# A two-block graph attention kernel: the last two chunks' share of conv2's scores made apart from the features

## The chip, the cores and the metric

One core of one Trainium2 chip. The metric is the device time of one execution in microseconds (us). The kernel before has a median of 359.05 us over three runs (358.48, 359.05, 359.10); smaller is better.

## The reference, cut to what matters

256 nodes with 768 features, 4096 edges and a self loop for each node. Block 0 is two attention convolutions, conv1 with 8 heads of 768 channels and conv2 with one head; a layer norm and block 1 (two more convolutions with residual products) follow.

```python
def gat_conv(x, src, dst, W, a_src, a_dst, b, heads, out_ch):
    h = (x @ W).reshape(n, heads, out_ch)
    alpha_src = jnp.einsum('nhc,hc->nh', h, a_src)
    alpha_dst = jnp.einsum('nhc,hc->nh', h, a_dst)
    e = leaky_relu(alpha_src[src] + alpha_dst[dst], 0.2)
    p = jnp.exp(e - segment_max(e, dst)[dst])
    alpha = p / segment_sum(p, dst)[dst]
    return segment_sum(h[src] * alpha[:, :, None], dst).reshape(n, heads * out_ch) + b
# block 0
h = elu(gat_conv(x, src, dst, W1, a_src1, a_dst1, b1, 8, 768))
out = gat_conv(h, src, dst, W2, a_src2, a_dst2, b2, 1, 768)
x = layernorm(x + out)
```

W1 is 768 x 6144 and W2 is 6144 x 768, in float32. The scores alpha_src and alpha_dst of conv2 are dot products of each row of h @ W2 with a vector of 768; such a dot product can also be taken as h times (W2 times the vector), for all rows of W2 or for some of them.

## The kernel before, in words

**Number format.** Every large product takes three passes over operands split in a high part (rounded to fp32r) and a low part (what is left): high x high, high x low, low x high. ScalarE makes the high part by a copy and a following engine subtracts it from the source for the low part.

**Weights.** SyncE loads pairs of 128-row chunks of 768 columns into the three groups of `raw` (`load_phase`, L540; its issue L538). ScalarE splits a chunk into `ring_hi` (`split_hi`, L349, issued at L357), GpSimd makes `ring_lo` (`split_lo`, L367, issued at L370). A group is loaded again once GpSimd is done with its second chunk. A phase is six chunks: phase 2h-1 holds head h's part of W1 (phase 0 head 0's), phase 2h head h-1's part of W2, and phase 15, the last of block 0, head 7's part of W2. `split_hi` waits for a free ring slot, `chunk_used` counting the chunks that TensorE is done with.

**A head.** For head h TensorE projects x on six chunks (`project_chunk`, L1026), VectorE takes the two score dots from PSUM (L1515), TensorE broadcasts the source scores (`scores`, L1049), ScalarE and VectorE make the softmax, TensorE transposes the weights (L1075) and aggregates transposed features (`aggregate_T`, L1091, issued at L1096). `elu` (ScalarE L787, VectorE L1646) turns that in three parts of two chunks into zT: ScalarE relu (L794) and exp (L800), VectorE L1657, ScalarE `zT_hi` (L808), VectorE `zT_lo` (L1666). TensorE adds zT times the part of W2 into three PSUM banks that hold conv2's projected features of all heads so far (`accumulate`, L1039). The first projected chunk of head h+1 writes PSUM's third bank only after part 0 of head h's elu is out of it (`bank2_wait` in `project_chunk`, on `z_lo_done`). Heads 2 to 7 are loops or copies of a loop; heads 0 and 1 and ScalarE's head 7 are written out.

**The accumulator banks.** Tile 0 (nodes 0 to 127) has its columns 0:512 in the first bank and 512:768 in the second, tile 1 its columns 0:256 in the second and 256:768 in the third. In `product` (L999) a tile is two pieces, so a chunk costs six matmuls per tile: three of 512 columns and three of 256.

**The end of block 0.** After head 7's aggregation TensorE adds phase 15's six chunks to tile 0, then the 512-column pieces of tile 1, then its 256-column pieces (`last_accumulate`, L1241 to L1265). Behind each of these VectorE takes the dots (L1515, L1764). Then come `scores` (L1060), twelve matmuls of zeros (`keep_warm`, L1024, called at L1271), the leaky relu (ScalarE L764, VectorE L1571), the mask and row maximum (L1581), the exponential (ScalarE L773), its product with the edge counts (L1594), the transposed weights (`weights_tiles`, L1087; split by ScalarE L785 and VectorE L1643), and `aggregate` (L1118, issued at L1130), tile by tile and in each tile first the 512 columns, then the 256. Its results are scaled and summed on VectorE (`y_piece`, L1795), centred (ScalarE L907, VectorE L1805), transposed on TensorE (L1282), split (ScalarE L913, VectorE `x1_lo` L1788), and block 1's first products begin (`wide_product`, L1298). ScalarE converts features with `projected_tile_hi` (L738), VectorE with `conv2_lo` (L1750). Block 1's weights go through the same ring in 40 chunks of a written plan (`chunks_hi` L379, `split_lo1` L386).

**Rows for later.** Seven vectors of block 1 are loaded over all partitions behind the edge counting (L574, L576, semaphore `rows_loaded`); one of them is split into `bias_rows` by ScalarE (L883) and VectorE (L1756) after head 7. Both inputs of L1756 lie in SBUF. Most other VectorE instructions with two tensors read at least one from PSUM.

## Time and profile before

| what | value |
|---|---|
| median of three runs | 359.05 us |
| the profiled execution, its own time | 358.43 us |
| its span in the trace | 356.6 us |
| TensorE busy | 347.9 us (98%) |
| GpSimd busy | 242.4 us (68%) |
| ScalarE busy | 218.5 us (61%) |
| VectorE busy | 213.4 us (60%) |
| conv2's last products, first to last | 242.56 to 255.56 us |
| conv2's aggregation begins | 260.70 us |

The span is what the trace covers; the execution's own time is 1.83 us longer. TensorE's records are matmuls in a pipeline, so the start of one to the start of the next is its price and its listed duration is longer than that. Matmuls on zeros count as busy. In a timeline a line gives start, duration, engine and the line of the kernel; the bracket is the idle time before it and what ended it.

### The profile page before, as it was taken

To read this page: it belongs to the slowest core of one execution; us is meant where nothing else is said; L and a number is where in the kernel's file an instruction comes from. 1 tells how busy PE (TensorE), PEld (TensorE's weight loads), DVE (VectorE), ACT (ScalarE), POOL (GpSimd) and SP (SyncE) were. 2 spreads that over 40 slices of the span, in tenths; PEclk is the share of its full clock that TensorE was granted. 3 is DMA by queue.
4 is the path that set the end of the run, shared out by engine and by line. 5 is a ranking of instruction groups with operands and counts; after the bars stand their busy time and mean duration, and the time that the engine had idled before them with its cause. 6 is when DMAs were issued, how large, how long until landed. Compare 5 with 4: busy or idle time off the path is not lost.

```text
span 356.6 us, 6079 instructions
## 1 busy us (share of the span) xinstructions
PE 347.9 (98%) x2058; PEld 298.9 (84%) x2060; DVE 213.4 (60%) x545; ACT 218.5 (61%) x376; POOL 242.4 (68%) x163
## 2 busy tenths in 40 slices
PE   7999999999999999999999999999999999999994
PEld 4888889889888988988898898898667888788883
DVE  4999883263546418244552732636687897944776
ACT  5987697547737754864674575476376866255601
POOL 2379769657693884968569396674257898687911
PEclk9999999999999999999999999999999999999999
DMA  7987969576656556656574754757072656246002
GB/s 235 312 299 225 391 214 257 179 240 144 227 150 203 176 155 205 170 176 183 170 217 143 224 170 141 246 159 237 11 218 94 217 179 198 99 135 221 0 2 88
DMA packets 24544, 65.15 MB, mean 183 GB/s; under 512 B 1952, under 2 KB 3024, under 8 KB 24528
## 3 DMA queue, kind: packets, MB, share of 16 engines
q1 hardware_dynamic: 20864, 55.02, 47.0%
q10 hardware_dynamic: 3664, 9.92, 10.8%
q8 instruction: 9, 0.15, 0.2%
q14 instruction: 7, 0.06, 0.0%
HBM read 64.15 MB, written 0.79 MB: 182 GB/s over the span
## 4 chain that ended last, share of the span: by engine, by line
PE 92%; DVE 4%; ACT 1%; DMA 1%; issue 1%; DVEq 0%; SPq 0%
PE ps L1008 64%; PE ps L1298 10%; PE ps L1096 9%; PE ps L1130 2%; PE ps L1362 2%; PE ps L1075 1%; DMA x_sb<-in_x 1%; PE ps L1060 1%; PE ps L1192 1%; DVE stats L1744 1%; DVE ps L1964 1%; DVE z L1971 1%; PE ps L1157 0%; PE ps L1383 0%; PE ps L1310 0%
## 5 line engine op out<-in xcount | busy, mean ns | idle before, releaser
L370 POOL TENSOR_TENSOR ring_lo<-raw,ring_hi 128x768 fp32r<-128x768 f32 x92 | 167.0, 1849 | 70.9 <-ACT ring_hi L357 70.8
L357 ACT ACTIVATE ring_hi<-raw 128x768 fp32r<-128x768 f32 x96 | 77.3, 839 | 35.7 <-PE ps L1008 28.8
L386 POOL TENSOR_TENSOR ring_lo<-raw,ring_hi 128x512 fp32r<-128x512 f32 (+1 forms) x40 | 59.5, 1517 | 20.3 <-ACT ring_hi L379 20.2
L1008 PE MATMUL ps<-ring_hi,zT_hi 128*128 128x256 f32 (+1 forms) x256 | 69.3, 345 | 0.4 <-ACT zT_hi L808 0.4
L1008 PE MATMUL ps<-ring_lo,zT_hi 128*128 128x256 f32 (+1 forms) x256 | 67.1, 337 | 0.0
L1008 PE MATMUL ps<-ring_hi,zT_lo 128*128 128x256 f32 (+1 forms) x256 | 66.8, 338 | 0.0
L1515 DVE CUSTOM_DVE_ANT_0 e<-ps,att 128x768 f32<-128x768 f32 x38 | 34.3, 953 | 47.6 <-PE ps L1008 47.6
L1008 PE MATMUL ps<-ring_hi,xT_hi 128*128 128x512 f32 x192 | 51.2, 343 | 0.3 <-ACT xT_hi L702 0.3
L1008 PE MATMUL ps<-ring_lo,xT_hi 128*128 128x512 f32 x192 | 50.0, 336 | 0.0
L1008 PE MATMUL ps<-ring_hi,xT_lo 128*128 128x512 f32 x192 | 49.8, 337 | 0.0
L1008 PEld LDWEIGHTS ps<-ring_lo,zT_hi 128*128 128x128 f32 x256 | 43.0, 188 | 5.6
L1008 PEld LDWEIGHTS ps<-ring_hi,zT_lo 128*128 128x128 f32 x256 | 43.0, 188 | 5.5
L1008 PEld LDWEIGHTS ps<-ring_hi,zT_hi 128*128 128x128 f32 x256 | 42.0, 189 | 6.4 <-ACT zT_hi L808 1.0
L379 ACT ACTIVATE ring_hi<-raw 128x512 fp32r<-128x512 f32 (+1 forms) x40 | 26.5, 712 | 17.0 <-PE ps L1008 10.0
L1657 DVE SCALAR_TENSOR_TENSOR ps<-ps,b_plus,z 128x256 f32<-128x256 f32 x48 | 21.2, 487 | 25.9 <-ACT z L800 25.8
L1008 PEld LDWEIGHTS ps<-ring_hi,xT_hi 128*128 128x128 f32 x192 | 32.3, 188 | 5.0 <-ACT xT_hi L702 0.7
L1008 PEld LDWEIGHTS ps<-ring_lo,xT_hi 128*128 128x128 f32 x192 | 32.7, 188 | 4.2
L1008 PEld LDWEIGHTS ps<-ring_hi,xT_lo 128*128 128x128 f32 x192 | 32.6, 188 | 4.1
L1096 PE MATMUL ps<-pT_hi,h_hi 128*128 128x256 f32 x96 | 26.0, 282 | 0.0
L1096 PE MATMUL ps<-pT_hi,h_lo 128*128 128x256 f32 x96 | 26.0, 282 | 0.0
L1666 DVE SCALAR_TENSOR_TENSOR zT_lo<-ps,zT_hi 128x512 fp32r<-128x512 f32 x24 | 16.6, 691 | 15.3 <-ACT zT_hi L808 15.3
L794 ACT ACTIVATE z<-ps,b_minus 128x256 f32<-128x256 f32 x48 | 20.1, 471 | 6.2 <-PE ps L1096 6.2
(172 smaller groups left out, 545.4 us busy)
## 6 DMA issues: line engine op xcount, KB each, us to landing
raw<-in_L_gnn_W SPq DMA_DIRECT2D x54, 768.0 KB, 4.5
raw<-in_L_gnn_Wr SPq DMA_DIRECT2D x8, 768.0 KB, 4.3
att<-in_L_gnn_a_src ACTq DMA_DIRECT2D x10, 384.0 KB, 4.0
att<-in_L_gnn_a_dst ACTq DMA_DIRECT2D x10, 384.0 KB, 5.2
raw<-in_L_gnn_W SPq DMA_DIRECT2D x4, 384.0 KB, 5.0
x_sb<-in_x SPq DMA_DIRECT2D x3, 256.0 KB, 4.8
...
```

The lines of the kernel that those rows point to most:

```text
L357: eng.activation(slot_hi(c), raw_chunk(c), ACT.Copy).then_inc(hi_done, 1)
L370: eng.tensor_tensor(slot_lo(c), raw_chunk(c), slot_hi(c).bitcast(F32), ALU.subtract)\
L379: eng.activation(ring_hi[:, q["ring_at"]:q["ring_at"] + w], raw[:, q["raw_group"], q["raw_at"]:q["raw_at"] + w], ACT.Copy)\
L386: eng.tensor_tensor(ring_lo[:, q["ring_at"]:q["ring_at"] + w], raw[:, q["raw_group"], q["raw_at"]:q["raw_at"] + w], ring_hi[:, q["ring_at" ...
L794: act.activation(z[:, t * N:(t + 1) * N], ps[:, at:at + N], ACT.Relu, bias=b1_minus[:, bass.ds(KD * h + t, 1)], scale=-1.0).then_inc(elu_r ...
L1008: last = pe.matmul(ps[:, at + to:at + to + hi - lo], a, b[:, lo:hi], start=start and n == 0 and to != D, stop=stop and n == PASSES - 1, sk ...
L1096: return pe.matmul(ps[:, at:at + N], feat(features, 0, j)[:, ch:ch + P], weights_part[:, 0, j, :], start=first, stop=final, skip_group_che ...
L1130: return pe.matmul(ps[:, nat_at[i] + lo:nat_at[i] + hi], weights_part[:, 0, j, i * P:(i + 1) * P], feat(features, a, j)[:, lo:hi], start=f ...
L1298: last = pe.matmul(ps[:, to:to + HW], a, b, start=k == 0 and n == 0, stop=k == KD - 1 and n == PASSES - 1, skip_group_check=True)
L1515: dve.tensor_tensor_reduce(junk[:, at:at + w], of[:, (k - first_head(a)) * w:(k - first_head(a) + 1) * w], att[:, half_at * row + k * w:ha ...
L1657: dve.scalar_tensor_tensor(ps[:, at:at + N], ps[:, at:at + N], b1_plus[:, bass.ds(KD * h + t, 1)], z[:, t * N:(t + 1) * N], ALU.add, ALU.m ...
L1666: dve.scalar_tensor_tensor(zT_lo[:, 2 * q:2 * q + 2, :].rearrange("p k n -> p (k n)"), ps[:, at:at + 2 * N], -1.0, hi.bitcast(F32), ALU.ad ...
```

## The change

Chunks 4 and 5 of phase 15 get a second way into the scores. GpSimd multiplies these two raw chunks with the two attention vectors spread over the partitions (`weigh_rows`, four instructions of 128 x 768), ScalarE sums their rows (`row_sum`, four), and the four columns are split and multiplied with zT (`late_rows`), turned into columns (`late_columns`) and added to the dots that VectorE takes from the accumulator after chunks 0 to 3 (`ends`). TensorE then adds chunks 4 and 5 bank by bank around the broadcast of the scores. The twelve matmuls of zeros go. conv2's aggregation is ordered by feature tile instead of by column piece. The attention vectors are loaded a second time, early, by SyncE. The split of `bias_rows` moves from behind head 7 to head 1.

The diff, without declarations, with the leading eight spaces and some plain lines left out:

```diff
+att2 = hs[:, 0:2 * D]
+ZV_AT, ZV_COLS_AT = 0, N
+LATE = (KD - 2, KD - 1)
...
+def weighted_row(m):
+    at = 2 * N + (m % 2) * D
+    return am[:].rearrange("p a b c -> p (a b c)")[:, at:at + D]
...
+def src_col(a, k, j):
+    if isinstance(a, int) and a == A_CONV2 and j == 0:
+        return ends[:, 0:1]
+    return a_s[:, pair(a, k, j)]
+def dst_col(a, k, i):
+    if isinstance(a, int) and a == A_CONV2 and i == 0:
+        return ends[:, 1:2]
+    return a_d[:, pair(a, k, i)]
...
+    sp.wait_ge(unpacked, 2)
+    for n, v in enumerate((b0_as2, b0_ad2)):
+        sp.dma_start(att2[:, n * D:(n + 1) * D], v[0:1, :].partition_broadcast(P)).then_inc(att2_loaded, 16)
     with sp.Fori(2, H0) as h:
         load_phase(2 * h - 1, w1_of(h))
         load_phase(2 * h, w2_of(h - 1))
...
-    with pool.Fori(1, H0) as h:
+    with pool.Fori(1, H0 - 1) as h:
         head(h)
+    def weigh_rows(c):
+        for half_at in range(2):
+            m = 2 * LATE.index(c) + half_at
+            if m >= 2:
+                pool.wait_ge(attw_done, m - 1)
+            pool.tensor_tensor(weighted_row(m), raw_chunk(c), att2[:, half_at * D:(half_at + 1) * D], ALU.mult)\
+                .then_inc(weighted_done, 1)
+    phase_lo(PHASES - 2)
+    pool.wait_ge(raw_full[LATE[0] // 2], 16 * PHASES)
+    pool.wait_ge(att2_loaded, 32)
+    weigh_rows(LATE[0])
+    for c in range(LATE[0]):
+        split_lo(pool, PHASES - 1, c)
+    weigh_rows(LATE[1])
+    for c in LATE:
+        split_lo(pool, PHASES - 1, c)
...
+        if last:
+            after_exps(h, between=lambda: (row_sum(0), row_sum(1)))
+            elu(h, between=lambda: row_sum(2))
+            row_sum(3)
+        else:
+            after_exps(h)
+            elu(h)
+    def row_sum(m):
+        act.wait_ge(weighted_done, m + 1)
+        act.activation(weighted_row(m), weighted_row(m), ACT.Copy, scale=SLOPE - 1.0 if m % 2 else 1.0,
+                       accum_out=attw[:, m:m + 1]).then_inc(attw_done, 1)
+    def after_exps(h, between=None):
         for c in range(4):
             split_hi(act, 2 * h + 1, c)
         weights_hi(h)
+        if between is not None:
+            between()
         for c in (4, 5):
             split_hi(act, 2 * h + 1, c)
...
     att_for(2)
+    act.wait_ge(rows_loaded, 16 * 7)
+    for half_at in range(2):
+        act.activation(bias_rows[half_at], rows_hc[0:BIAS_ROWS, 3, half_at * HW:(half_at + 1) * HW], ACT.Copy)\
+           .then_inc(bias_row_hi, 1)
     elu(1)
     with act.Fori(2, H0 - 1) as h:
         head(h)
     head(H0 - 1, last=True)
-    act.wait_ge(rows_loaded, 16 * 7)
-    for half_at in range(2):
-        act.activation(bias_rows[half_at], rows_hc[0:BIAS_ROWS, 3, half_at * HW:(half_at + 1) * HW], ACT.Copy)\
-           .then_inc(bias_row_hi, 1)
+    act.wait_ge(attw_done, 4)
+    act.activation(attw_hi[:, :], attw[:, :], ACT.Copy).then_inc(attw_hi_done, 1)
     act.wait_ge(xb_done, NT)
     act.dma_start(rows_d[:, 3, :], b1_br2.partition_broadcast(P)).then_inc(rows_loaded, 16)
...
-    act.wait_ge(a_dst_done, before(A_CONV2) + 1)
-    projected_tile_hi(A_CONV2, 0)
+    act.wait_ge(zv_rows_ps, 1)
+    act.activation(zv_rows[:, :], ps[0:2, ZV_AT:ZV_AT + N], ACT.Copy).then_inc(zv_rows_done, 1)
     chunks_hi(0, 2)
     leaks(A_CONV2)
+    chunks_hi(2, 3)
+    exps(A_CONV2, (0, 1))
+    act.wait_ge(tile0_done, 1)
+    projected_tile_hi(A_CONV2, 0)
+    weights_tiles_hi(A_CONV2)
+    act.wait_ge(chunk_used, CH * PHASES)
+    act.wait_ge(h_lo0_done, before(A_CONV2) + 1)
     projected_tile_hi(A_CONV2, 1)
-    exps(A_CONV2, (0, 1))
-    chunks_hi(2, 3)
     load_att(A_GAT1A, b1_as1.rearrange("h c -> (h c)"), b1_ad1.rearrange("h c -> (h c)"), HC)
-    weights_tiles_hi(A_CONV2)
...
     pe.wait_ge(z_lo_done, 3 * (H0 - 1) + 1)
     for c in (0, 1):
         last_accumulate(c, 0, passes=LAST_ONE)
-    for q in (1, 2):
-        pe.wait_ge(z_hi_done, 3 * (H0 - 1) + q + 1)
-        for c in (2 * q, 2 * q + 1):
-            chunk(PHASES - 1, c)
-            last_accumulate(c, 0, passes=FIRST_TWO)
-        pe.wait_ge(z_lo_done, 3 * (H0 - 1) + q + 1)
-        for c in (2 * q, 2 * q + 1):
-            last = last_accumulate(c, 0, passes=LAST_ONE)
+    pe.wait_ge(z_hi_done, 3 * (H0 - 1) + 2)
+    for c in (2, 3):
+        chunk(PHASES - 1, c)
+        last_accumulate(c, 0, passes=FIRST_TWO)
+    pe.wait_ge(z_lo_done, 3 * (H0 - 1) + 2)
+    for c in (2, 3):
+        last = last_accumulate(c, 0, passes=LAST_ONE)
+    last.then_inc(early_bank_done, 1)
+    for c in range(LATE[0]):
+        last = last_accumulate(c, 1, piece=0)
+    last.then_inc(early_bank_done, 1)
+    def late_rows():
+        pe.wait_ge(z_lo_done, 3 * H0)
+        pe.wait_ge(attw_lo_done, 1)
+        for c in LATE:
+            at = 2 * LATE.index(c)
+            for n, (a, b) in enumerate(three(attw_hi[:, at:at + 2], attw_lo[:, at:at + 2],
+                                             zT_hi[:, c, :], zT_lo[:, c, :])):
+                last = pe.matmul(ps[0:2, ZV_AT:ZV_AT + N], a, b, start=c == LATE[0] and n == 0,
+                                 stop=c == LATE[1] and n == PASSES - 1)
+        last.then_inc(zv_rows_ps, 1)
+    def late_columns():
+        pe.wait_ge(zv_rows_done, 1)
+        for i in range(NT):
+            at = ZV_COLS_AT + 2 * i
+            last = pe.transpose(ps[:, at:at + 2], zv_rows[:, i * P:(i + 1) * P], ident[0:2, 0:2])
+        last.then_inc(zv_ps, 1)
+    for c in range(LATE[0]):
+        if c == 2:
+            late_rows()
+        if c == 3:
+            late_columns()
+        last_accumulate(c, 1, piece=1).then_inc(chunk_used, 1)
+    pe.wait_ge(partial_done, 2)
+    for c in LATE:
+        chunk(PHASES - 1, c)
+        if c == LATE[1]:
+            last_accumulate(c, 0, piece=0, passes=(0,))
+            scores(A_CONV2)
+            last_accumulate(c, 0, piece=0, passes=(1, 2))
+        else:
+            last_accumulate(c, 0, piece=0)
+    pe.wait_ge(partial_done, 4)
+    pe.wait_ge(a_dst_done, before(A_CONV2) + 1)
+    for c in LATE:
+        last_accumulate(c, 0, piece=1)
+        last = last_accumulate(c, 1, piece=0)
     last.then_inc(tile0_done, 1)
-    for c in range(CH):
-        last = last_accumulate(c, 1, piece=1)
-    last.then_inc(wide_piece_done, 1)
-    pe.wait_ge(h_lo0_done, before(A_CONV2) + 1)
-    for c in range(CH):
-        last_accumulate(c, 1, piece=0).then_inc(chunk_used, 1)
-    pe.wait_ge(z_lo_done, 3 * H0)
-    idle = PROJ + BANK
-    scores(A_CONV2)
-    keep_warm(12, idle)
+    pe.wait_ge(a_dst_done, before(A_CONV2) + 2)
+    for c in LATE:
+        last_accumulate(c, 1, piece=1).then_inc(chunk_used, 1)
+    def aggregate_conv2():
+        def part(i, j, weights_part, features, first, final):
+            done = None
+            for lo, hi in NAT_PIECES:
+                done = pe.matmul(ps[:, NAT_AT[i] + lo:NAT_AT[i] + hi], weights_part[:, 0, j, i * P:(i + 1) * P],
+                                 feat(features, A_CONV2, j)[:, lo:hi], start=first, stop=final)
+                if final:
+                    done.then_inc(conv2_done, 1)
+        for i in range(NT):
+            pe.wait_ge(wt_hi_done, i + 1)
+            pe.wait_ge(h_hi_done, before(A_CONV2) + 1)
+            if i == 1:
+                pe.wait_ge(h_lo0_done, before(A_CONV2) + NT)
+            part(i, 0, pT_hi, h_hi, True, False)
+            pe.wait_ge(h_lo0_done, before(A_CONV2) + 1)
+            part(i, 0, pT_hi, h_lo, False, False)
+            pe.wait_ge(wt_lo_done, i + 1)
+            part(i, 0, pT_lo, h_hi, False, False)
+            pe.wait_ge(h_hi_done, before(A_CONV2) + NT)
+            part(i, 1, pT_hi, h_hi, False, False)
+            part(i, 1, pT_lo, h_hi, False, False)
+            pe.wait_ge(h_lo0_done, before(A_CONV2) + NT)
+            part(i, 1, pT_hi, h_lo, False, True)
     weights_tiles(A_CONV2)
-    aggregate(A_CONV2)
+    aggregate_conv2()
...
     weights_lo(1)
+    dve.wait_ge(bias_row_hi, 2)
+    for half_at in range(2):
+        row = bias_rows[half_at][32:33, :]
+        dve.tensor_tensor(row, rows_hc[32:33, 3, half_at * HW:(half_at + 1) * HW], row.bitcast(F32),
+                           ALU.subtract).then_inc(bias_row_done, 1)
     elu(1)
     with dve.Fori(2, H0) as h:
...
+    conv2_sum_done = (a_src_done, a_dst_done)
+    def piece_dots(i, cols, initial, to, done):
+        of = source_at(A_CONV2, i)[:, cols]
+        for half_at in range(2):
             junk = (e1, e2)[half_at][:].rearrange("p a b c -> p (a b c)")
-            to = partial[:, half_at:half_at + 1] if initial is None else t[:, 1:2]
-            dve.tensor_tensor_reduce(junk[:, D + cols.start:D + cols.stop], of,
+            dve.tensor_tensor_reduce(junk[:, i * D + cols.start:i * D + cols.stop], of,
                                      att[:, half_at * D + cols.start:half_at * D + cols.stop],
                                      SLOPE - 1.0 if half_at else 1.0,
                                      0.0 if initial is None else initial[:, half_at:half_at + 1],
-                                     ALU.mult, ALU.add, to).then_inc(done[half_at], 1)
-    tile_dots(A_CONV2, 0)
-    conv2_lo(0)
-    dve.wait_ge(wide_piece_done, 1)
-    piece_dots(slice(N, D), None, (partial_done, partial_done))
-    projected(A_CONV2, 1)
+                                     ALU.mult, ALU.add, to[half_at]).then_inc(done[half_at], 1)
+    dve.wait_ge(att_loaded, 32 * (A_CONV2 + 1))
+    dve.wait_ge(early_bank_done, 1)
+    piece_dots(0, slice(0, BANK), None, [partial[:, n:n + 1] for n in (4, 5)], (partial_done, partial_done))
+    dve.wait_ge(attw_hi_done, 1)
+    dve.tensor_tensor(attw_lo[:, :], attw[:, :], attw_hi[:, :].bitcast(F32), ALU.subtract).then_inc(attw_lo_done, 1)
+    dve.wait_ge(early_bank_done, 2)
     dve.wait_ge(partial_done, 2)
-    piece_dots(slice(0, N), partial, (a_src_done, a_dst_done))
+    piece_dots(0, slice(BANK, D), partial[:, 4:6], [partial[:, n:n + 1] for n in (0, 1)], conv2_sum_done)
+    piece_dots(1, slice(0, N), None, [partial[:, n:n + 1] for n in (2, 3)], (partial_done, partial_done))
+    dve.wait_ge(a_src_done, before(A_CONV2) + 1)
+    dve.wait_ge(a_dst_done, before(A_CONV2) + 1)
+    dve.wait_ge(partial_done, 4)
+    dve.wait_ge(zv_ps, 1)
+    dve.tensor_tensor(ends[:, :], ps[:, ZV_COLS_AT:ZV_COLS_AT + 4], partial[:, 0:4], ALU.add).then_inc(zv_added, 1)
+    dve.wait_ge(zv_added, 1)
+    dve.wait_ge(chunk_used, CH * (PHASES - 1) + LATE[0])
+    piece_dots(1, slice(N, D), ends[:, 2:4], [t[:, 1:2] for t in (a_s, a_d)], conv2_sum_done)
     masked_scores(A_CONV2)
     weigh(A_CONV2, 0)
     weigh(A_CONV2, 1)
-    conv2_lo(1)
+    conv2_lo(0)
     weights_tiles_lo(A_CONV2)
     inverse_sums(A_CONV2)
+    conv2_lo(1)
```

## Rows read from the trace of the kernel before

**Rows 1.** Chain of waits, end of block 0: start us, us, what

```profile
242.56 13.01 PE ps L1008 x72
...
256.23 0.42 PE ps L1060 x2
...
259.70 0.45 PE ps L1087 x2
...
260.70 4.43 PE ps L1130 x24
```

**Rows 2.** Table of windows: busy us of each engine, clock, DMA share, GB/s

```profile
255.56:260.70 5.14, 3.76 (x17) 1.77 (x19) 3.92 (x15) 3.44 (x8) 2.04 (x3) 1.00 0.10 37
```

**Rows 3.** Timeline of TensorE, conv2's last products

```profile
249.10 0.39 PE L1008 MATMUL ps<-ring_hi,zT_hi 128*128 128x512 f32 x1
...
253.21 0.32 PE L1008 MATMUL ps<-ring_hi,zT_hi 128*128 128x256 f32 x1
```

**Rows 4.** Timeline of ScalarE, head 7 up to its elu

```profile
232.92 3.05 ACT L357 ACTIVATE ring_hi<-raw 128x768 fp32r<-128x768 f32 x4 [0.50 <-issue]
...
236.35 0.83 ACT L357 ACTIVATE ring_hi<-raw 128x768 fp32r<-128x768 f32 x1
...
239.33 0.84 ACT L794 ACTIVATE z<-ps,b_minus 128x256 f32<-128x256 f32 x2 [0.58 <-PE ps L1096]
```

**Rows 5.** Timeline of GpSimd, phase 15

```profile
233.84 10.88 POOL L370 TENSOR_TENSOR ring_lo<-raw,ring_hi 128x768 fp32r<-128x768 f32 x6 [5.48 <-ACT ring_hi L357]
```

**Rows 6.** Tile raw, 225 to 245 us: SyncE's issues, time to landing

```profile
L538 SPq DMA_DIRECT2D raw<-in_L_gnn_W x2: 368/373/378, 224.8 to 228.4; - x2
...
DMA to landing us min/median/max: 4.2/4.4/4.6
```

**Rows 7.** Timeline of VectorE, end of block 0

```profile
253.41 0.69 DVE L1764 CUSTOM_DVE_ANT_0 e<-ps,att 128x512 f32<-128x512 f32 x1 [0.32 <-PE ps L1008]
...
259.95 0.95 DVE L1750 TENSOR_TENSOR h_lo<-ps,h_hi 128x768 fp32r<-128x768 f32 x1
...
264.46 0.76 DVE L1795 SCALAR_TENSOR_TENSOR ps<-ps,rz,x_sb 128x512 f32<-128x512 f32 x1
...
266.41 1.01 DVE L1788 TENSOR_TENSOR xT_lo<-ps,xT_hi 128x512 fp32r<-128x512 f32 x2
```

**Rows 8.** Timeline of ScalarE, conv2's features and weights

```profile
257.40 0.81 ACT L738 ACTIVATE h_hi<-ps 128x768 fp32r<-128x768 f32 x1
...
260.17 0.77 ACT L785 ACTIVATE pT_hi<-ps 128x256 fp32r<-128x256 f32 x2
```

**Rows 9.** Timeline of ScalarE: head 1 up to its elu; later the bias rows

```profile
50.31 3.04 ACT L357 ACTIVATE ring_hi<-raw 128x768 fp32r<-128x768 f32 x4
...
56.54 0.89 ACTq L685 DMA_DIRECT2D att<-in_L_gnn_a_dst  x1
57.59 0.84 ACT L794 ACTIVATE z<-ps,b_minus 128x256 f32<-128x256 f32 x2 [0.22 <-PE ps L1096]
...
246.76 0.62 ACT L883 ACTIVATE zT_hi<-rows_hc 33x512 fp32r<-33x512 f32 x1
```

**Rows 10.** Timeline of VectorE, part 0 of head 1's zT_lo

```profile
60.68 0.69 DVE L1666 SCALAR_TENSOR_TENSOR zT_lo<-ps,zT_hi 128x512 fp32r<-128x512 f32 x1 [0.67 <-ACT zT_hi L808]
```

**Rows 11.** Timeline of TensorE: head 1's aggregation, head 2 in the third bank

```profile
55.97 0.28 PE L1096 MATMUL ps<-pT_hi,h_hi 128*128 128x256 f32 x1
...
61.67 0.39 PE L1008 MATMUL ps<-ring_hi,xT_hi 128*128 128x512 f32 x1
```

**Rows 12.** DMA issues from 35 to 40 us (KB each, us to landing)

```profile
raw<-in_L_gnn_W SPq DMA_DIRECT2D x1, 768.0 KB, 11.3
```

**Rows 13.** Table of windows, 40 to 42 us (columns as in rows 2)

```profile
40.00:42.00 2.00, 2.00 (x17) 1.90 (x17) 1.88 (x5) 1.74 (x5) 1.92 (x2) 1.00 1.02 411
```

**Rows 14.** Timeline of VectorE, the bias rows behind head 7

```profile
247.93 0.68 DVE L1756 TENSOR_TENSOR zT_hi<-rows_hc,zT_hi 1x512 fp32r<-1x512 f32 x1 [0.34 <-ACT zT_lo L883]
```

**Rows 15.** Timeline of GpSimd, head 1

```profile
47.48 14.63 POOL L370 TENSOR_TENSOR ring_lo<-raw,ring_hi 128x768 fp32r<-128x768 f32 x8 [5.56 <-ACT ring_hi L357]
```

51 lines of the change are left out of this document (22 added, 29 removed).

## The prediction

> **What bounds the kernel now.** I read the page first: TensorE is busy 98% of the span, so only two kinds of time can be won, TensorE's gaps and work that TensorE does for nothing. The chain of waits shows where it is not TensorE that counts [rows 1]: conv2's last products run 13.0 us without a break, then between the last of them (255.56) and the aggregation (260.70) the chain goes through VectorE's last dots, the broadcast of the scores, the softmax and the transposes. The table of windows for that stretch [rows 2] says that TensorE was busy 3.76 of 5.14 us, but the work that counts there is six transposes, 0.42 + 0.45 us [rows 1]; the rest of the busy time is zeros. So about 4.3 us are open, and the most that a better order can give is that.
>
> **What the change puts in the gap.** The prices of TensorE's instructions are distances of starts [rows 3]: from 249.10 to 253.21 there are 18 matmuls of 512 columns, 0.228 us each, and 18 matmuls of 256 columns follow up to the end of the products at 255.56, at most 0.13 us each; without the longer end of the last one it is 0.122. The dots need chunks 0 to 3 only. What is left behind the third bank's chunk 3 is chunks 4 and 5: 12 x 0.228 + 12 x 0.122 = 4.2 us. That is the cover; I follow each step to see whether it holds. All times are on the clock of the profiled execution.
>
> *The start.* ScalarE gets two row sums between the weights of head 7 and its splits of chunks 4 and 5. Splits follow one another every (3.05 - 0.83) / 3 = 0.74 us and the next one began at 236.35; relu began at 239.33 [rows 4]. Two row sums and two splits take 4 x 0.74 = 2.96 us and end at 239.31, just in time. What a row sum's accumulator costs is on no row; VectorE's read of its own is listed with 0.08 to 0.14 us, so I take 0.12 each, between 0 and 0.3: elu and with it the first product come 0.25 us late.
>
> *GpSimd.* It was idle for 5.48 us before phase 15 [rows 5]. The third group was issued at 228.4 and takes 4.3 us to land [rows 6], so the first two multiplications can start at 232.75. I price a multiplication like a split of the same shape, 10.88 / 6 = 1.81 us: both are done at 236.4, splits 0 to 3 at 243.7, the other two multiplications at 247.3, splits 4 and 5 at 249.1 and 251.0. TensorE wants chunk 3 at 242.8 + 12 x 0.175 = 244.9 (0.175 is the mean of the two prices, as a chunk has both pieces) and chunks 4 and 5 at 252.5 and 253.2, so nothing waits, with one microsecond to spare. The last row sum is then ready at about 248.3 and its split at 249.4; `late_rows` is reached at 242.8 + 24 x 0.175 + 12 x 0.122 + 6 x 0.228 = 249.8. This is the tightest point (margin 0.4).
>
> *Scores.* `late_rows` adds 6 x 0.122 = 0.7 us and `late_columns` two transposes of two columns, at 0.1 to 0.2 us each, plus a wait of some 0.15 for ScalarE's copy. The third bank's chunk 3 ends at 252.7. The dot of 512 columns takes 0.69 us [rows 7]; TensorE does four matmuls meanwhile and waits 0.1 us. The scores are broadcast at 253.6 and not 256.23, so weights come at 259.70 - 2.6 = 257.1. TensorE's products end at 242.8 + 12.84 (the 13.01 less the 0.17 by which a last end lies behind the next start) + 0.7 for the rows + 0.3 for the columns + 0.3 of waits + 0.44 for the broadcast = 257.4. The softmax is hidden, and the transposes begin at 257.4 instead of 259.70: 2.3 us gained here.
>
> *The aggregation.* Here part of it is given back. Before, one copy and one low part of the features lay before the gap and the rest in it. Now all are behind the products: ScalarE copies a tile in 0.81 us and splits two weight tiles in 0.77 [rows 8], VectorE needs 0.95 per low part [rows 7], and the second copy waits for the first low part. From the transposes: weights split 258.3, low part of tile 0 258.7, copy of tile 1 259.6, low part of tile 1 260.6. The passes of tile 0 hang on these and end at about 261.1; tile 1 follows with six passes of 0.35 us and ends at 263.2 against 265.1 [rows 1]. Also, both column pieces of a tile now end together, so VectorE begins tile 1's sum only 0.35 + 0.15 us earlier than the last product's end: at about 263.2 where it was 264.46 [rows 7]. The end of `x1_lo` is what block 1's first products wait for, and it moves as this does. If the copies of this chain follow closer than I think the gain is 1.6 us, if looser 0.9. I take 1.3 us. Behind it the chain is nearly all TensorE (92% of the whole chain), so the 1.3 us reach the end. The zeros cost nothing and their removal gives nothing by itself: they ended before the transposes.
>
> **The bias rows.** ScalarE's two copies (0.62 each, overlapping by 0.1 as the splits do) and VectorE's two subtractions move before head 1's elu. Behind head 7 they were hidden. In head 1 ScalarE's last issue of a DMA ended at 57.43 and relu began at 57.59 [rows 9], so relu moves to 57.45 + 2 x 0.52 = 58.5, 0.9 us later. The exponential and VectorE's two steps are a chain behind it. Part 0 of `zT_lo` ended at 61.37 [rows 10], and TensorE's first matmul on the third bank, which needs it, began at 61.67 [rows 11]: 0.30 us of slack, of which 0.05 to 0.15 is the semaphore's. TensorE stalls 0.65 us there (between 0.5 and 0.9), and as it works without gaps until head 7 nothing gives that back.
>
> **The second load of the attention vectors.** Two more transfers of 384 KB stand on SyncE's queue ahead of phase 3's first group, which landed 11.3 us after its issue because the queue was full [rows 12]; at 411 GB/s [rows 13] 0.79 MB are 1.9 us more. Group 0 then lands at 38.5 + 11.3 + 1.9 = 51.7; group 1, which follows it in the full queue, some 1.8 us later at 53.5. ScalarE's four splits began at 50.31 and ended at 53.35 [rows 9]; they now end at 55.1, the copy of the weights at 55.6. TensorE began the aggregation that wants it at 55.97 [rows 11]. I cost that at nothing, with 0.3 us left; at 1 us more delay it is 0.7. The wait for `unpacked` costs nothing, it is over before SyncE gets there. Declarations and GpSimd's unrolled head cost nothing that TensorE waits for.
>
> **Sum.** 358.43 - 1.3 + 0.65 = 357.8 on the profiled execution. That run was 0.62 us under the median, so on the median 358.4. A measurement tells 0.2% (0.72 us) from no change: the forecast is at the upper edge of what cannot be told. The range of this case alone is 357.8 to 359.1.
>
> **Rivals.**
> *1. VectorE and GpSimd get in each other's way (slower).* The moved subtractions read two tensors from SBUF. Behind head 7 they took 0.68 us with GpSimd idle [rows 14]; in head 1 GpSimd works from 47.48 without a break for 14.6 us on operations of 1.83 us that read SBUF too [rows 15]. No row has such a VectorE instruction beside a running GpSimd one. If each has to wait for one to end, the pair is late by 1 to 3.5 us, all of it ahead of head 1's elu; `attw_lo`, which also reads two tensors from SBUF while GpSimd splits chunk 4, can be late by up to 1.8 us with `late_rows` behind it, beyond the margin of 0.4. Stall in head 1: 1.3 to 3 us instead of 0.65, plus 0 to 1.4 in conv2. Taking 2.3 and 0.6: 359.05 - 1.3 + 2.3 + 0.6, about 360.6; it decides from 0.65 us of extra wait on. Its range is 359.3 to 361.5. For it: the type of operand; against it: no row shows one being held up. The Trainium skill (SBUF — State Buffer, section "SBUF: two separate sides") says just this: a VectorE instruction with two SBUF inputs and a GpSimd instruction that reads SBUF share a port pair as an exclusive lock, and whoever comes second is blocked for a whole instruction. The traces here neither confirm nor deny it. Chance 0.30.
> *2. The front costs nothing (faster).* ScalarE may reach the bias rows early or the chain behind relu be shorter than listed. Then the 1.3 us stand alone, up to 1.6: 357.75. The timeline is against it. Chance 0.17.
> *3. The gain fails in conv2.* The accumulator reads, the last row sum or the tile-wise chain of copies cost more: the scores come later than the products end, or tile 0's passes are late. With 1 us of the 1.3 lost: 359.4. Chance 0.13.
> The forecast keeps 0.40.
>
> **Numbers.** Of the forecast's 0.40 some 0.16 is faster by over 0.2%, 0.24 within. Rival 2 is faster; rival 1 gives 0.25 slower and 0.05 within; rival 3 0.09 within and 0.04 slower. Rounded: faster 0.34, within 0.37, slower 0.29. The range runs from rival 2 with its larger gain, 357.2, to the middle of rival 1, 360.6.
>
> **What would show it.** In the profile after: the scores' broadcast at about 253.6 + 0.65; transposes with no idle time before them; gaps of 0.1 to 0.5 us inside tile 0's aggregation; relu of head 1 near 58.5 and TensorE's stall on the third bank of 0.5 to 0.9 us (rival 2: none; rival 1: over 1.3, with VectorE's L1756 starting or lasting past its 0.68). I am wrong if `late_rows` waits for `attw_lo`, if head 1's aggregation starts late, or if block 1's first product comes less than 0.3 us or more than 2 us earlier relative to head 7's aggregation.

## The result: slower by 1.3%, and the profile after

The changed kernel takes 363.24 us (median of four runs, 362.24 to 365.08) where the kernel before, on the same chip, takes 359.03: a ratio of 1.0130 with a 95% interval of 1.0113 to 1.0147. The forecast was 358.4 with a range up to 360.6, so both the size and the direction were wrong. The profiled execution took 365.08 us with a span of 363.4. It is the longest of the four, 6.65 us over the profiled one of before, and the sums below are made on it.

| what | before | after |
|---|---|---|
| profiled execution, own time / span | 358.43 / 356.6 us | 365.08 / 363.4 us |
| mean granted TensorE clock of that execution | 1.000 | 0.988 |
| head 1's aggregation begins | 55.97 | 56.78 |
| first matmul on the third bank behind it | 61.67 | 65.94 |
| head 2's aggregation begins | 86.16 | 93.10 |
| conv2's last products begin | 242.56 | 249.58 |
| block 1's first product | 266.26 | 272.70 |

From head 1's aggregation on, the differences of the two columns are +0.81, +4.27, +6.94, +7.02 and +6.44. All of the loss is there when head 2's aggregation begins, at a quarter of the span; the end of block 0, which the change is about, gives 0.58 us back. The view to read first is therefore the list of TensorE's waits (kernel after; total us, times, longest):

```profile
PE ps L1083 <- DVE zT_lo L1794: 3.2, 1, 3.2
...
PE ps L1337 <- DVE attw_lo L1903: 0.8, 1, 0.8
PE ps L1171 <- ACT pT_hi L835: 0.6, 1, 0.6
```

The first is the third bank's matmul of head 2 waiting for head 1's elu, the second `late_rows` waiting for the low part of the four columns, the third head 1's aggregation waiting for its weights. The timeline of the kernel after in head 1 (start us, us) shows where the first comes from; it answers to [rows 9 to 11, 15]:

```profile
53.56 11.71 POOL L393 TENSOR_TENSOR ring_lo<-raw,ring_hi 128x768 fp32r<-128x768 f32 x6 [2.40 <-ACT ring_hi L380]
...
52.64 1.58 ACT L380 ACTIVATE ring_hi<-raw 128x768 fp32r<-128x768 f32 x2 [2.22 <-DMA raw<-in_L_gnn_W]
54.57 1.58 ACT L380 ACTIVATE ring_hi<-raw 128x768 fp32r<-128x768 f32 x2 [0.35 <-DMA raw<-in_L_gnn_W]
...
58.22 0.61 ACT L947 ACTIVATE zT_hi<-rows_hc 33x512 fp32r<-33x512 f32 x1
...
59.26 0.81 ACT L850 ACTIVATE z<-ps,b_minus 128x256 f32<-128x256 f32 x2
...
64.57 0.60 ACT L864 ACTIVATE zT_hi<-ps 128x512 fp32r<-128x512 f32 x1 [3.11 <-DVE ps L1785]
...
59.38 1.99 DVE L1855 TENSOR_TENSOR zT_hi<-rows_hc,zT_hi 1x512 fp32r<-1x512 f32 x1 [2.02 <-ACT zT_lo L947]
61.30 2.32 DVE L1855 TENSOR_TENSOR zT_lo<-rows_hc,zT_lo 1x512 fp32r<-1x512 f32 x1
63.65 0.89 DVE L1785 SCALAR_TENSOR_TENSOR ps<-ps,b_plus,z 128x256 f32<-128x256 f32 x2
65.19 0.69 DVE L1794 SCALAR_TENSOR_TENSOR zT_lo<-ps,zT_hi 128x512 fp32r<-128x512 f32 x1 [0.66 <-ACT zT_hi L864]
...
65.94 0.79 PE L1083 MATMUL ps<-ring_hi,xT_hi 128*128 128x512 f32 x1 [3.23 <-DVE zT_lo L1794]
```

The two subtractions of the bias rows, one partition by 512, take 1.99 and 2.32 us; behind head 7 the first took 0.68 [rows 14]. GpSimd is at work beside them without a break (53.56 to 65.27). Read one by one, its splits show who waits for whom: the first subtraction ends at 61.37, 0.55 us after the split that ran when it began (60.82), the second at 63.62, 0.55 us after the next one (63.07). And the two splits that start meanwhile last 2.28 and 2.24 us where the others of this stretch last 1.83 to 1.86. elu's first step on VectorE stands behind them, and TensorE behind elu. The steps of elu themselves keep their price (0.69 for L1794, as in [rows 10]), and they run beside the same GpSimd instructions.

What follows the wait is in the table of windows of the kernel after (us of the stretch, busy of PE, PEld, DVE, ACT, POOL, granted clock, DMA share, GB/s):

```profile
62.00:64.00 2.00, 0.71 (x6) 0.46 (x4) 1.97 (x2) 0.00 (x0) 2.00 (x2) 1.00 0.94 343
64.00:66.00 2.00, 0.06 (x1) 0.06 (x1) 1.34 (x4) 1.43 (x4) 1.28 (x1) 0.69 0.84 341
66.00:68.00 2.00, 2.00 (x5) 1.61 (x6) 1.34 (x4) 1.52 (x4) 0.00 (x0) 0.50 0.68 207
68.00:70.00 2.00, 2.00 (x9) 1.71 (x8) 1.34 (x4) 1.14 (x2) 0.00 (x0) 0.50 0.54 215
70.00:72.00 2.00, 2.00 (x9) 1.69 (x8) 0.18 (x1) 0.72 (x2) 1.73 (x1) 0.60 0.04 15
72.00:74.00 2.00, 2.00 (x13) 1.78 (x12) 0.00 (x0) 0.62 (x2) 1.71 (x2) 1.00 0.00 0
...
64.77:71.59 6.82, 5.65 (x16) 4.75 (x17) 3.66 (x7) 4.21 (x9) 1.83 (x2) 0.50 0.50 182
```

TensorE stood idle for 3.2 us, and when it begins again the granted clock is 0.50, the lower of its two levels (1.2 GHz). The last line is that whole stretch, 6.8 us, of which TensorE works 5.65. Busy reads 2.00 in the windows of 2 us all the same: only the count of matmuls (5 and 9 in place of 13) tells. From the third bank's first matmul to head 2's aggregation it takes 27.16 us and took 24.49: 2.7 us that no wait lists, and near half of the 5.65.

At the end of block 0 (timeline of the kernel after, answering to [rows 1, 7, 8]):

```profile
243.98 0.19 ACT L890 ACTIVATION_READ_ACCUMULATOR am<-am 128x1 f32 x1
...
254.00 3.64 POOL L393 TENSOR_TENSOR ring_lo<-raw,ring_hi 128x768 fp32r<-128x768 f32 x2
...
255.75 1.91 DVE L1903 TENSOR_TENSOR attw_lo<-attw,attw_hi 128x4 fp32r<-128x4 f32 x1
...
257.81 0.28 PE L1337 MATMUL ps<-zT_hi,attw_hi 128*2 128x256 f32 x1 [0.84 <-DVE attw_lo L1903]
...
261.42 0.32 PE L1135 MATMUL ps<-ident,ends 128*128 128x128 f32 x1
...
264.98 0.76 PE L1162 MATMUL ps<-ident,e 128*128 128x128 f32 x4
265.83 0.62 PE L1379 MATMUL ps<-h_hi,pT_hi 128*128 128x512 f32 x2
266.55 0.62 PE L1379 MATMUL ps<-h_lo,pT_hi 128*128 128x512 f32 x2
```

A subtraction of four columns lasts 1.91 us. Behind it everything goes as meant: the scores are broadcast (261.42) while products still run, there is no idle time before the transposes (264.98), the aggregation follows right behind them, and from the first of the last products to block 1's first product 23.12 us in place of 23.70, the wait of 0.84 included.

Theory 1 after this reading: a VectorE instruction with both inputs in SBUF is held up while GpSimd works. That makes the stall of 3.2 us and the 0.84 us before `late_rows`, and the idle TensorE loses its clock on top. The rivals: the loss comes from the second load's delay or from ScalarE's copies; it is the size of the instruction and not its operands that costs; and, for the clock, that it costs nothing of its own. Each expectation below stands as it was written before its run.

### The profile page after: what moved, and what is told of

It is laid out like the page before. It is cut to its first block, busy times and chain, and to the rows that moved or that the text cites. A ratio compares the mean times of both kernels' runs of the same rounds, so it can differ in the third digit from the quotient of the medians.

```text
span 363.4 us, 6088 instructions
## 1 busy us (share of the span) xinstructions
PE 351.2 (97%) x2056; PEld 300.5 (83%) x2056; DVE 218.6 (60%) x551; ACT 222.2 (61%) x386; POOL 250.6 (69%) x167
## 2 busy tenths in 40 slices
DMA packets 24833, 65.94 MB, mean 181 GB/s; under 512 B 1985, under 2 KB 3057, under 8 KB 24817
## 4 chain that ended last, share of the span: by engine, by line
PE 74%; DVE 8%; ACT 6%; issue 4%; POOL 4%; DMA 3%; ACTq 0%; DVEq 0%; SPq 0%; POOLq 0%
PE ps L1083 51%; PE ps L1426 9%; PE ps L1171 6%; POOL ring_lo L393 3%; ACT ring_hi L380 2%; PE ps L1490 2%; DMA raw<-in_L_gnn_W 1%; PE ps L1150 1%; DMA x_sb<-in_x 1%; PE ps L1135 1%; ACT h_hi L794 1%; DVE e L1643 1%; DVE stats L1877 1%; PE ps L1379 1%; DVE zT_lo L1855 1%
## 5 line engine op out<-in xcount | busy, mean ns | idle before, releaser
L1083 PE MATMUL ps<-ring_hi,zT_lo 128*128 128x512 f32 (+1 forms) x256 | 67.3, 338 | 0.0
L1643 DVE CUSTOM_DVE_ANT_0 e<-ps,att 128x768 f32<-128x768 f32 x36 | 32.4, 953 | 49.7 <-PE ps L1083 49.7
L1083 PE MATMUL ps<-ring_hi,xT_hi 128*128 128x512 f32 x192 | 52.4, 349 | 3.2 <-DVE zT_lo L1794 3.2
L1083 PE MATMUL ps<-ring_lo,xT_hi 128*128 128x512 f32 x192 | 50.9, 341 | 0.0
L1083 PE MATMUL ps<-ring_hi,xT_lo 128*128 128x512 f32 x192 | 50.7, 342 | 0.0
L1083 PEld LDWEIGHTS ps<-ring_hi,xT_hi 128*128 128x128 f32 x192 | 33.2, 193 | 8.6 <-DVE zT_lo L1794 3.4
L1794 DVE SCALAR_TENSOR_TENSOR zT_lo<-ps,zT_hi 128x512 fp32r<-128x512 f32 x24 | 16.6, 692 | 15.3 <-ACT zT_hi L864 15.3
L864 ACT ACTIVATE zT_hi<-ps 128x512 fp32r<-128x512 f32 x24 | 14.4, 598 | 14.8 <-DVE ps L1785 14.7
```

What stands on the lines that cost most here:

```text
L864: act.activation(zT_hi[:, 2 * q:2 * q + 2, :].rearrange("p k n -> p (k n)"), ps[:, at:at + 2 * N], ACT.Copy, bias=-1.0).then_inc(z_hi_done, 1)
L1083: last = pe.matmul(ps[:, at + to:at + to + hi - lo], a, b[:, lo:hi], start=start and n == 0 and to != D, stop=stop and n == PASSES - 1, sk ...
L1643: dve.tensor_tensor_reduce(junk[:, at:at + w], of[:, (k - first_head(a)) * w:(k - first_head(a) + 1) * w], att[:, half_at * row + k * w:ha ...
L1794: dve.scalar_tensor_tensor(zT_lo[:, 2 * q:2 * q + 2, :].rearrange("p k n -> p (k n)"), ps[:, at:at + 2 * N], -1.0, hi.bitcast(F32), ALU.ad ...
```

## The experiments

All ratios are against the kernel before on the same chip, whose median was 358.64 us in the runs of the first four, 358.63 in those of the next four and 358.83 in those of the last three.

**1. Only the bias rows moved, on the kernel before.**

```diff
-    (behind head 7) act: 2 x activation(bias_rows ...);  dve: 2 x tensor_tensor(row, rows_hc, row, subtract)
+    (head 1, before elu(1)) the same four instructions
```

> The kernel before with one part of the change alone: the split of the bias rows moved to head 1. Theory 1 (a VectorE instruction that reads two tensors from SBUF is held up by each running GpSimd instruction): L1756's two instructions last about 2 us each instead of 0.68, TensorE stalls 2.5 to 3.5 us at head 2's first chunk, and where the granted clock falls after it another 1 to 3 us go; time 361.5 to 365. Theory 2 (only the copies' 1.04 us delay relu, the forecast's term): both instructions stay at 0.7 us, stall 0.65 us, time about 359.7.

Measured 363.92 us (363.78 to 364.74), ratio 1.0153 (1.0137 to 1.0169). The timeline of VectorE:

```profile
58.69 2.18 DVE L1727 TENSOR_TENSOR zT_hi<-rows_hc,zT_hi 1x512 fp32r<-1x512 f32 x1 [3.31 <-ACT zT_lo L878]
60.80 2.30 DVE L1727 TENSOR_TENSOR zT_lo<-rows_hc,zT_lo 1x512 fp32r<-1x512 f32 x1
```

This move alone makes 5.3 us, more than the whole loss of 4.2. TensorE's wait on the third bank is 3.6 us.

**2. Only the second load of the attention vectors, on the kernel before.**

```diff
+    sp.wait_ge(unpacked, 2)
+    for n, v in enumerate((b0_as2, b0_ad2)): sp.dma_start(att2[...], ...)
     with sp.Fori(2, H0) as h:
```

> The kernel before with the second load of the attention vectors alone, early in SyncE's order. Theory 1 (the transfers in front delay phase 3's first groups past the slack): ScalarE's copy of head 1's weights ends about 0.8 us later than TensorE wants it, aggregation of head 1 starts 0.5 to 0.9 us late, time 359.6 to 359.9. Theory 2 (the forecast: inside the slack): no idle time before head 1's aggregation, time 359.0 within 0.3.

Measured 358.79 us (358.39 to 359.72), ratio 1.0009 (1.0000 to 1.0019). Head 1's aggregation begins at 55.99, as before. In the profile head 2's begins 0.34 us later than before (86.50 against 86.16), the median is 0.15 us up: alone the load costs little.

**3. The change with its front put back.** The bias rows are copied behind head 7 and subtracted by GpSimd after its third chunk of block 1; the second load stands before phase 15.

```diff
-    (head 1) act: 2 copies of bias rows;  dve: 2 subtractions
+    (behind attw_hi) act: 2 copies
+    pool (between chunks of block 1): 2 x tensor_tensor(row, rows_hc, row, subtract)
-    sp: att2 load before Fori(2, H0)
+    sp: att2 load before load_phase(PHASES - 1, ...)
```

> The changed kernel with both costs at the front taken out: the bias rows are copied behind head 7 and subtracted by GpSimd after its third chunk of block 1, the second load of the attention vectors stands before phase 15. Theory 1 (the whole loss lies in head 1, conv2 itself gains 0.6 us and pays 0.8 us for attw_lo): time 358.2 to 358.7, faster than before by 0.4 to 0.8. Theory 2 (the change also loses elsewhere, in block 1 or in the clock): 359.5 or more.

Measured 358.49 us, but from 357.46 to 359.69 over twelve runs; ratio 0.9992 (0.9978 to 1.0006). That is the time that theory 1 named, and the loss is gone; but against the kernel before on the same chip it is 0.15 us and not told from no change. In its profile `attw_lo` fell on the seam between two splits of GpSimd, which worked from 247.70 to 251.36 without a break:

```profile
247.70 3.66 POOL L393 TENSOR_TENSOR ring_lo<-raw,ring_hi 128x768 fp32r<-128x768 f32 x2
...
249.46 0.16 DVE L1906 TENSOR_TENSOR attw_lo<-attw,attw_hi 128x4 fp32r<-128x4 f32 x1
```

0.16 us here and 1.91 in the kernel after, for the same instruction at the same distance (6.17 us) from the first of the last products. In both kernels it is listed 0.06 us before the second split (249.51 here, 255.81 there). So at such a seam the listed times do not tell which of the two gets in first, and 1.75 us hang on it. Whether this makes the spread of 2.2 us was not seen, as no longer execution was profiled.

**4. The same, and ScalarE makes `attw_lo`.** ScalarE computes scale times input plus a bias per partition, one column at a time.

```diff
-    dve.tensor_tensor(attw_lo, attw, attw_hi, ALU.subtract)
+    for m in range(4):
+        act.activation(attw_lo[:, m:m + 1], attw_hi[:, m:m + 1], ACT.Identity, bias=attw[:, m:m + 1], scale=-1.0)
```

> As c_front_back, and the low part of the four weight columns is made by ScalarE (identity of minus the high part plus the column as bias) so that VectorE has no instruction with two SBUF inputs there. Theory 1: attw_lo no longer holds up VectorE for 1.9 us, TensorE's wait of 0.8 us before late_rows goes, time 0.7 to 0.9 us under c_front_back (357.4 to 357.8). Theory 2 (late_rows would have waited for the last row sum anyway): less than 0.3 us under c_front_back.

Measured 357.55 us (357.44 to 357.72), ratio 0.9970 (0.9958 to 0.9981): faster than both kernels, 1.1 us under before, with a spread of 0.28 us over six runs. From the first of the last products (242.76) to block 1's first product (264.89) it takes 22.13 us, 1.57 less than before; the latter comes 1.37 earlier. In experiment 3's profile, where `attw_lo` took its 0.16 us, that stretch took 22.14 us too, so the 0.94 us between the two medians lie in executions that no profile shows. That `attw_lo` makes them is the likely reading and not a shown one. TensorE's waits of this kernel behind the start:

```profile
PE ps L1095 <- ACT zT_hi L872: 0.5, 1, 0.5
PE ps L1095 <- ACT xT_hi L766: 0.3, 1, 0.3
...
PE ps L1422 <- ACT x_sb L994: 0.2, 1, 0.2
```

**5. The instruction by itself.** The kernel before with small VectorE instructions on idle tiles: in head 1 twice while GpSimd works, and once near the end, where it is idle (eleven in all).

```diff
+    dve.tensor_tensor(hs[512 columns], counts, far, ALU.add)           # two inputs in SBUF (L1727)
+    dve.tensor_tensor(hs[4 columns], counts, far, ALU.add)             # the same, 4 columns (L1728)
+    dve.tensor_scalar(hs[512 columns], counts, 1.0, None, ALU.add)     # one input (L1729)
+    dve.tensor_tensor(hs[512 columns], ps, counts, ALU.add)            # one in PSUM, not near the end (L1731)
```

> The kernel before with twelve small VectorE instructions added that compute nothing the output needs: a 128x512 sum of two SBUF tensors, a 128x4 sum of two SBUF tensors, a 128x512 add of a constant to one SBUF tensor and a 128x512 sum of one PSUM and one SBUF tensor, twice in head 1 while GpSimd works without a break, and the first three once near the end while GpSimd is idle. The time is no question here, the durations are. Theory 1 (the operands decide): beside GpSimd the two sums of SBUF tensors last until the running GpSimd instruction ends, 0.2 to 1.9 us longer than alone, the 4 column one as long as the 512 column one; the sum with a PSUM tensor keeps 0.69 us. Theory 2 (size decides, or it is the single partition of L1756): the 4 column sum stays at 0.2 us and the 512 column one near 0.7 us.

The tile's instructions (least, median, greatest ns), then the timelines of VectorE and GpSimd in head 1:

```profile
L1727 DVE TENSOR_TENSOR hs<-counts,far x3: 686/1112/1595, 52.7 to 346.6; 128x512 f32<-128x512 f32 x3
L1728 DVE TENSOR_TENSOR hs<-counts,far x3: 157/1754/1799, 53.7 to 347.2; 128x4 f32<-128x4 f32 x3
L1729 DVE TENSOR_SCALAR hs<-counts x3: 411/414/422, 55.5 to 347.3; 128x512 f32<-128x512 f32 x3
L1731 DVE TENSOR_TENSOR hs<-ps,counts x2: 675/676/676, 55.8 to 60.0; 128x512 f32<-128x512 f32 x2
```

```profile
52.69 1.11 DVE L1727 TENSOR_TENSOR hs<-counts,far 128x512 f32<-128x512 f32 x1
53.73 1.80 DVE L1728 TENSOR_TENSOR hs<-counts,far 128x4 f32<-128x4 f32 x1
55.45 0.41 DVE L1729 TENSOR_SCALAR hs<-counts 128x512 f32<-128x512 f32 x1
55.78 0.68 DVE L1731 TENSOR_TENSOR hs<-ps,counts 128x512 f32<-128x512 f32 x1
...
47.64 15.91 POOL L371 TENSOR_TENSOR ring_lo<-raw,ring_hi 128x768 fp32r<-128x768 f32 x8 [6.07 <-ACT ring_hi L358]
```

The execution took 366.26 us with its additions, a number that stands for nothing else. Four columns take 0.16 us with GpSimd idle and 1.75 to 1.80 beside it. So neither size nor the single partition decides but the operands: the same kind of instruction with one input in PSUM takes 0.68 beside GpSimd. Each of the two held sums of four columns ends 0.02 us after the split that ran beside it (55.53 after 55.50, 59.77 after 59.75): it waits for that split's end. GpSimd pays too: its eight splits took 15.91 us, and [rows 15] has 14.63. The splits that start while a sum of 512 columns waits last 2.30 and 2.24 us in place of some 1.85.

The instruction with a single SBUF input took 0.41 throughout; but it stood right behind one that had just waited for GpSimd, so these rows don't exclude that it would wait elsewhere. It isn't free for GpSimd either: the splits that begin 0.02 us after it last 2.07 and 2.06 us and end 1.67 to 1.68 us after it ends, as the others end 1.66 to 1.70 after a two-input one. It seems to hold GpSimd up as these do; no run has it alone.

**6. Only ScalarE's two copies in head 1**, the subtractions left behind head 7.

```diff
+    (head 1, before elu(1)) act: 2 x activation(bias_rows ...)
```

> The kernel before with ScalarE's two copies of the bias rows alone moved to head 1; VectorE subtracts behind head 7 as before. This is the forecast's own term for head 1. Theory 1 (relu 0.9 us later against 0.3 us of slack): TensorE stalls 0.5 to 0.9 us at head 2's first chunk in the third bank, time 0.4 to 0.9 us over before. Theory 2 (the chain takes it up): no stall, time within 0.2 of before.

Measured 359.96 us (359.70 to 360.15), ratio 1.0035 (1.0022 to 1.0048). Timeline of TensorE:

```profile
62.85 0.50 PE L1008 MATMUL ps<-ring_hi,xT_hi 128*128 128x512 f32 x1 [0.46 <-DVE zT_lo L1666]
```

The stall is 0.46 us, near the 0.65 that the prediction gave to the move; the time rose by 1.3. In this profile head 1's aggregation already begins 0.55 us late (56.52), behind longer waits for `ring_lo` and x. From there to the third bank's first matmul it takes 6.33 us and took 5.70, which is 0.63 more, and to head 2's aggregation 0.80 more. So the copies' price is between 0.5 and 1.3 us and not settled closer. The subtractions take the rest of the 5.3, about 4.

**7. The kernel before without its twelve matmuls of zeros.**

```diff
     scores(A_CONV2)
-    keep_warm(12, idle)
```

> The kernel before without the twelve matmuls of zeros between the scores and the transposes. Theory 1 (idle time of about 4 us lets the granted clock fall to 1.2 GHz, as the 3.2 us stall in the changed kernel did): conv2's aggregation and block 1's first products run at the lower clock for some us, time 1.5 to 4 us over before. Theory 2 (the forecast: the zeros cost and bring nothing): granted clock 1.00 in that stretch, time within 0.2 of before.

Measured 360.95 us (360.23 to 361.69), ratio 1.0065 (1.0053 to 1.0077). TensorE's wait before the transposes, and the table of windows:

```profile
PE ps L1087 <- DVE e L1593: 3.1, 1, 3.1
...
258.00:260.00 2.00, 0.00 (x0) 0.00 (x0) 1.87 (x9) 1.48 (x4) 0.00 (x0) 1.00 0.00 0
260.00:262.00 2.00, 1.81 (x7) 1.29 (x8) 1.93 (x6) 1.93 (x5) 1.44 (x2) 0.83 0.75 240
262.00:264.00 2.00, 2.00 (x7) 1.61 (x7) 0.21 (x1) 0.80 (x2) 2.00 (x2) 0.50 1.05 298
264.00:266.00 2.00, 2.00 (x11) 1.78 (x10) 1.62 (x6) 0.24 (x1) 1.60 (x2) 0.82 0.95 347
```

The wait before the transposes grows to an idle time of 3.1 us and the clock is at half behind it, for 3.4 us (261.30 to 264.72). Work that computes nothing was worth 2.3 us there by the medians, and 1.6 in this profile, the shortest of the six. The change can drop it only because its order closes the gap.

**8. Kernel 4 with the aggregation by column piece**, as it was before.

```diff
-    aggregate_conv2()      # tile by tile; tile 0's passes wait for tile 0's operands alone
+    by_piece()             # waits for both feature tiles, then 512 columns, then 256
```

> d_no_shared_port with conv2's aggregation in the order of the kernel before (512 columns, then 256, in each tile) instead of by feature tile. Theory 1 (the order by feature tile uses the time until the second copy and its low part are there): the aggregation starts about 1 us later and ends 0.5 to 0.9 us later, time 0.3 to 0.9 us over d_no_shared_port. Theory 2 (both wait for the same last low part): time within 0.2 of d_no_shared_port.

Measured 358.50 us (357.69 to 359.82), ratio 0.9998 (0.9984 to 1.0013). Timeline of TensorE:

```profile
259.79 0.50 PE L1419 MATMUL ps<-h_hi,pT_hi 128*128 128x512 f32 x1 [1.72 <-ACT h_hi L802]
```

From the first of the last products (242.90) to block 1's first product (265.40) it takes 22.50 us, only 0.4 more than kernel 4's 22.13, yet the median is 0.95 us up: of the twelve runs those of 357.7 to 358.0 us have a mean clock of 0.997 to 0.999, those of 359.0 to 359.8 one of 0.992 to 0.994. The profile is one of the short ones, so that the clock falls behind the idle time of 1.7 us is an inference from the means. If it holds, the order by tile is worth having for the idle time that it takes away, more than for its own 0.4.

**9, 10. Zeros in the stall of experiment 1, and its control.** Head 2 of TensorE is written out, so that zeros can stand there alone.

```diff
+    for _ in range(14):     # only in the first of the two, just ahead of the third bank's first matmul
+        pe.matmul(ps[:, PROJ:PROJ + BANK], zeros[:, 0:P], zeros[:, :], start=False, stop=False)
```

> a_bias_early (the kernel before with the bias rows' split in head 1, 363.92 us, stall 3.6 us, granted clock 0.50 for some 3 us behind it) with head 2 written out and 14 matmuls of 512 columns of zeros, added to an open accumulator of TensorE's own, put just ahead of the first matmul on the third bank, where TensorE stood idle. They take 14 x 0.228 = 3.2 us. Theory 1 (stall and falling clock are two costs: the stall's 3.3 us and 1.5 to 2.5 us of half clock behind it): the granted clock stays at 1.00, the wait for zT_lo shrinks to some 0.4 us while the third bank's first matmul starts at the same time as in a_bias_early, and the time is 361.6 to 362.6 us. Rival (the clock costs nothing of its own, since TensorE waits for VectorE and GpSimd afterwards anyway): the time is that of k_peeled, within 0.4 us.

> The control of j_zeros_in_stall: a_bias_early with head 2 written out and no zeros. Both theories: 363.5 to 364.5 us, a stall of 3.6 us and a granted clock of 0.50 in the 3 us behind it. If writing head 2 out costs or gives something of its own, it is seen here against 363.92.

Measured 363.41 us (362.59 to 364.19) with zeros, ratio 1.0122 (1.0100 to 1.0145), and 364.50 (363.86 to 364.95) without, ratio 1.0157 (1.0140 to 1.0174). Windows with zeros, then without:

```profile
64.00:66.00 2.00, 1.40 (x6) 0.59 (x5) 1.34 (x4) 1.72 (x4) 0.00 (x0) 1.00 0.83 296
66.00:68.00 2.00, 2.00 (x13) 1.73 (x12) 1.33 (x4) 1.25 (x3) 0.00 (x0) 1.00 0.32 128
68.00:70.00 2.00, 2.00 (x14) 1.73 (x13) 1.24 (x3) 1.42 (x3) 0.01 (x1) 1.00 0.02 6
```

```profile
64.00:66.00 2.00, 0.06 (x1) 0.06 (x1) 1.34 (x4) 1.43 (x4) 0.00 (x0) 1.00 0.86 284
66.00:68.00 2.00, 2.00 (x9) 1.68 (x10) 1.33 (x4) 1.53 (x4) 0.00 (x0) 0.84 0.41 164
68.00:70.00 2.00, 2.00 (x8) 1.78 (x7) 1.34 (x4) 1.14 (x2) 0.00 (x0) 0.50 0.00 0
```

The third bank's first matmul starts at 65.66 and at 65.94, and head 2's aggregation 24.73 and 26.27 us later (before: 24.49). So with the same delay and no falling clock 1.5 us are saved in the trace. The spans of the four executions of each are 360.8 to 361.2 and 362.1 to 363.2, in the middle 1.9 us apart. By the times it is 1.1 us, under the 1.9 or more that was expected, and their two intervals overlap: two of the four executions with zeros have 3.0 and 3.3 us outside their span where the other six have 1.8 to 1.9, and the reason was not found. The clock has a price of its own, seen in every span; its exact size in time is less sure.

**11. Kernel 4 with the second load early, as the change has it.**

```diff
-    sp: att2 load before load_phase(PHASES - 1, ...)
+    sp: att2 load before Fori(2, H0)
```

> d_no_shared_port with the second load of the attention vectors back where the change has it, ahead of phase 3. Alone on the kernel before this load cost 0.16 us (ratio 1.0009), in the profile of the kernel after head 1's aggregation began 0.8 us late. Theory 1 (the load is nearly free): 357.5 to 358.0 us, no wait of TensorE for pT_hi over 0.3 us. Rival (it costs what the profile of the kernel after shows): 358.2 to 358.6 us with head 1's aggregation starting at 56.5 or later.

Measured 358.20 us (357.59 to 359.90), ratio 0.9979 (0.9966 to 0.9993). Timeline of TensorE:

```profile
56.80 0.36 PE L1183 MATMUL ps<-pT_hi,h_hi 128*128 128x256 f32 x1 [0.53 <-ACT pT_hi L843]
```

Here the rival came out: head 1's aggregation begins 0.8 us late, as in the kernel after. The first group of phase 3 lands 14.5 us after its issue in the kernel after, 14.4 here, 13.4 in experiment 2 and 11.3 before [rows 12]. The 1.9 us that the prediction got from bytes and rate fit experiment 2 (2.1). They do not fit the 3.1 and 3.2 of the other two, and what makes the last 1.1 us was not found. The load costs between 0.1 and 0.65 us.

## Why the prediction was wrong

**The account of the profiled execution**, from its own time of before: 358.43 + 0.81 (head 1's aggregation late) + 3.46 (the third bank later still: the stall) + 2.67 (half clock up to head 2's aggregation) + 0.08 (row sums) - 0.58 (conv2) = 364.87. 0.2 us of 365.08 are left: block 1 takes 0.36 more and the time outside the span is 0.15 less. The 2.67 are near what the clock alone would make: TensorE worked 5.65 us at half of it, and half of that is 2.8.

*The bias rows: the step that failed.* The forecast's sum has a term for ScalarE's two copies and none for VectorE's two subtractions, which it took at the 0.68 us that they have with GpSimd idle [rows 14]. So it found a stall of 0.65 us. The subtractions took 1.99 and 2.32, the stall was 3.2. The copies were right: relu was forecast for 58.5 and began at 58.57 in experiment 1, without the late load, and at 59.26 in the kernel after, with it. Rival 1 had the mechanism and the place. Its price for the stall was too low, 1.3 to 3 us where 3.2 and 3.6 were measured; its price for `late_rows` was right, 0 to 1.4 us where it was 0.84. Its chance was 0.30 because no row of before showed it.

The Trainium skill (SBUF — State Buffer, section "SBUF: two separate sides") says that of a VectorE instruction with two SBUF inputs and a GpSimd instruction that reads SBUF the first has the shared ports for its whole length and the other is blocked. The rows here agree: 0.16 us against 1.80 for four columns, ending 0.02 us after GpSimd's split. That before has no such instruction beside GpSimd was no evidence against the rival; rival 1 ought to have been the forecast.

*The clock: a term that was missing.* Neither forecast nor rivals asked what a stall does to TensorE afterwards. Rival 1's own sum was 360.6; with the stall and `attw_lo` as measured (3.2 and 0.84 for 2.3 and 0.6) it would have been 361.8, still outside its range of 359.3 to 361.5. The clock and the late load lie in the rest up to 363.24; how they share it there isn't known, as the profiled execution is a longer one.

*The second load.* It was costed at nothing, and "at 1 us more delay it is 0.7". ScalarE's copy of the weights ended 1 us later than forecast (56.6 for 55.6), and head 1's aggregation began 0.8 us late. Alone the load cost 0.15 us, so the reading was at the edge, and the price given for the other side was right.

*conv2.* This was right, and in its steps: the broadcast was forecast 10.8 us behind the first product (253.6 less 242.8) and came at 11.0 once the 0.84 us are taken off (261.42 - 249.58 - 0.84); the transposes had no idle time before them; the accumulator's read stood with 0.19 us and moved the next instruction by 0.1 (0.12 was taken). The forecast gain of 1.3 us is 1.37 at block 1's first product in experiment 4, and 1.1 us of time. What took a part of it away in the change itself is `attw_lo`, named in rival 1. The chances of the forecast and its rivals add up to 0.33 faster and 0.38 within, where the prediction wrote 0.34 and 0.37; nothing hangs on it.

*The zeros.* "Cost nothing and their removal gives nothing" holds for the changed order alone; without it they bring 2.3 us (experiment 7), which the prediction did not see.
